# Cross-attention and FP8 layer on one core: ScalarE quantises the last three pieces, and TensorE turns the last four

## What is computed

```python
x = x + xattn(layernorm(x), ctx, ctx, ...)      # cross attention, an MLP of 512 hidden features, a layer norm
x = x + ffn(layernorm(x), weight, bias)         # one 128x128 layer; its input is rounded to 8-bit floats
...
f_diff = (v - attn @ v) @ W_diff.T + b_diff + q
h = layernorm(f_diff, ln_g, ln_b)
mlp = gelu(h @ W1.T + b1) @ W2.T + b2
out = layernorm(mlp + f_diff, ln_g, ln_b)
...
x_mat = quantize_e4m3(x2d).astype(float16)      # x2d: the second layer norm of the residual
out2d = x_mat @ w_mat.T + bias
```

## Time and profile before

| quantity | value |
|---|---|
| median of 3 runs | 262.22 us (261.59 to 262.32) |
| the profiled execution's own time | 262.39 us |
| its span in the trace | 260.6 us |
| VectorE busy | 225.0 us, 86% of the span |
| ScalarE busy | 214.1 us, 82% |
| TensorE matmuls busy | 209.4 us, 80% |
| GpSimd busy | 189.0 us, 73% |

### The profile page before, as it was taken

How to read it: one execution, slowest core, us unless ns; L and a number is a source line. 1 busy time by engine, 2 the same in 40 slices (tenths; PEclk the granted TensorE clock), 3 DMA queues, 4 the chain that set the end, 5 groups by cost and what they waited for, 6 DMA issues and landing times.

```text
span 260.6 us, 5926 instructions
## 1 busy us (share of the span) xinstructions
PE 209.4 (80%) x1723; PEld 178.2 (68%) x1723; DVE 225.0 (86%) x843; ACT 214.1 (82%) x774; POOL 189.0 (73%) x250
## 2 busy tenths in 40 slices
PE   2676696854499888887899999999999999996511
PEld 1754584633387666666699999999899999995400
DVE  2899999988879999999535889999999999999892
ACT  4599999998889999989997888989888776775431
POOL 2477666764899999991886796969697888666552
PEclk9999889895579999999999999999999999999855
DMA  5666554440000000000328189997978888977922
GB/s 146 193 201 192 171 150 136 144 118 1 1 0 3 3 0 3 1 3 4 40 26 95 19 96 135 122 132 111 149 117 132 131 123 127 140 121 121 103 62 60
DMA packets 51360, 23.65 MB, mean 91 GB/s; under 512 B 9856, under 2 KB 51200, under 8 KB 51328
## 3 DMA queue, kind: packets, MB, share of 16 engines
q0 software_dynamic: 15856, 7.87, 28.1%
q1 hardware_dynamic: 35040, 15.21, 21.8%
q10 hardware_dynamic: 432, 0.20, 0.4%
HBM read 9.37 MB, written 4.19 MB: 52 GB/s over the span
## 4 chain that ended last, share of the span: by engine, by line
POOL 28%; DVE 23%; ACT 20%; issue 13%; PE 11%; DMA 3%; SPq 0%; POOLq 0%; DVEq 0%; ACTq 0%
POOL F L407 7%; POOL xrstd L448 7%; ACT TQK L523 6%; ACT TQK L507 6%; POOL orstd L442 6%; DVE q_c L810 5%; POOL F L454 5%; DVE LN_c L818 5%; DVE F L838 5%; PE bank L1011 3%; ACT PV L518 3%; DMA LN_c<-in_ctx_dram 3%; ACT vT_c L512 2%; PE bank L960 1%; DVE F L863 1%
## 5 line engine op out<-in xcount | busy, mean ns | idle before, releaser
L1011 PEld LDWEIGHTS bank<-W2T,TQK 128*128 128x128 f32 x512 | 63.0, 191 | 6.7 <-DVE F L858 1.8
L1011 PE MATMUL bank<-W2T,TQK 128*128 128x128 f32 x512 | 64.8, 277 | 2.9 <-ACT TQK L545 2.9
L545 ACT ACTIVATE TQK<-bank,b1c 128x512 f32<-128x512 f32 (+1 forms) x68 | 42.8, 663 | 3.0 <-PE bank L1004 2.7
L448 POOL TENSOR_TENSOR xrstd<-xvar,pow_c 128x4 f32<-128x4 f32 (+1 forms) x17 | 18.6, 1092 | 22.6 <-DVE xvar L726 22.6
L362 POOL TENSOR_TENSOR xrstd<-xvar,pow_c 128x4 f32<-128x4 f32 x16 | 16.8, 1051 | 21.5 <-DVE xvar L726 21.5
L1002 PE MATMUL bank<-hTh,W1h 128*128 128x512 f32 (+1 forms) x68 | 30.0, 442 | 0.8 <-DVE hTl L801 0.8
L407 POOL DMA_DIRECT2D F<-rows x17 | 26.0, 1529 | 5.6 <-DVE E_c L796 5.6
L1003 PE MATMUL bank<-hTl,W1h 128*128 128x512 f32 (+1 forms) x68 | 26.0, 382 | 0.0
L1004 PE MATMUL bank<-hTh,W1l 128*128 128x512 f32 (+1 forms) x68 | 25.9, 381 | 0.0
L960 PE MATMUL bank<-WdT,vT_c 128*128 128x128 f32 x128 | 21.6, 321 | 4.5 <-ACT vT_c L512 4.3
L960 PEld LDWEIGHTS bank<-WdT,vT_c 128*128 128x128 f32 x128 | 18.8, 225 | 7.0 <-ACT vT_c L512 6.9
(11 more groups left out here) (129 smaller groups left out, 658.6 us busy)
## 6 DMA issues: line engine op xcount, KB each, us to landing
F<-rows POOLq DMA_DIRECT2D x29, 256.0 KB, 4.7
LN_c<-in_ctx_dram SPq DMA_DIRECT2D x16, 256.0 KB, 3.0
X<-in_x_dram SPq DMA_DIRECT2D x16, 256.0 KB, 3.2
out_dram<-F SPq DMA_DIRECT2D x15, 256.0 KB, 2.4
LN_c<-in_L_xattn_W_dram SPq DMA_DIRECT2D x1, 256.0 KB, 3.6
lT_c<-in_L_xattn_W_dram SPq DMA_DIRECT2D x1, 256.0 KB, 3.7
F<-rows POOLq DMA_DIRECT2D x2, 128.0 KB, 4.8
out_dram<-F SPq DMA_DIRECT2D x2, 128.0 KB, 1.8
```

Of the source, the lines that this page charges most:

```text
L448: pool.tensor_tensor(buf(xrstd, x1, G), buf(xvar, x1, G), pow_c[:, 0:x1.g], ALU.pow).then_inc(x1_rstd, 1)
L545: act.activation(hid(m, j), m1_bank(m, j), ACT.Gelu, bias=b1c[:, j:j + 1]).then_inc(gelu_ready, 1)
L1011: last = pe.matmul(M2_B[m.buf][:, i * D:(i + 1) * D], hid(m, j)[:, i * D:(i + 1) * D], W2T[:, j * D:(j + 1) * D], start=(j == 0 and i == 0 ...
```

## The change

Pieces 14 to 16 are quantised by ScalarE and not by VectorE: Identity with scale = rstd and bias = -mean * rstd, one activation a tile. The bias is made by a new GpSimd product `x1_shift` (into `nrden`, a buffer that is free in stage three, called `nmr`), behind each `x1_power`. VectorE's statistics of these pieces give the negative mean (`mean_sign` -1 in an operation that is there anyway). Two new semaphores, `xq_act` and `nmr_ready`, carry the new waits.

Piece 13 is turned by TensorE too (`XQ_HERE` goes from 14 to 13): its bf16 copy on ScalarE, its transposing DMA and the DMA's wait go. TensorE's turning now stands behind the MLP's products of the same step. It matters for piece 13 alone, since there is no MLP work in the later steps.

The new orders:

- ScalarE, last step: gelu(16, 0), gelu(16, 1), rounded(12), gelu(16, 2), gelu(16, 3), out_squares(15). After it: copy of turned 13, rounded(13), out_squares(16), quantise(14), copy of turned 14, quantise(15), rounded(14), copy of turned 15, quantise(16), rounded(15), copy of turned 16, rounded(16).
- VectorE, last step: output(15), residual(14), x1_stats(14), result(12). After it: output(16), residual(15), x1_stats(15), residual(16), x1_stats(16), result(13), result(14), result(15), result(16).
- GpSimd, last step: out_power(15). After it: x1_power(14), x1_shift(14), out_power(16), x1_power(15), x1_shift(15), add_bf(14), x1_power(16), x1_shift(16), add_bf(15), add_bf(16).

```diff
--- before.py
+++ after.py
@@ -91,7 +91,8 @@
     EARLY = 2
     NORMS = NC - 2
     BF_HERE = NP - 3
-    XQ_HERE = NP - 3
+    XQ_HERE = NP - 4
+    XQ_ACT = NP - 3
 
     with ExitStack() as ctx:
         def sb(name, shape, dt=F32):
@@ -174,6 +175,7 @@
         r16_c = LN_c[:, 2 * C:3 * C].bitcast(F16)
 
 
+        nmr = nrden
         qpart_c = RNORM[:, :]
         Wd_raw = E_c[:, 0:D]
         W1_raw, W1u = LN_c[:, 2 * C:2 * C + HB * D], LN_c[:, 3 * C:3 * C + HID]
@@ -289,6 +291,7 @@
             sem("x1_rstd"))
         xq_ready, xqT_ps, xqT_sb, ff_ps, r16_ready, y_ready = (
             sem("xq_ready"), sem("xqT_ps"), sem("xqT_sb"), sem("ff_ps"), sem("r16_ready"), sem("y_ready"))
+        xq_act, nmr_ready = sem("xq_act"), sem("nmr_ready")
         xq16_ready, xqT_in = sem("xq16_ready"), [sem(f"xqT_in{i}") for i in range(2)]
         stored, w1u_sb, wt_sb = sem("stored"), sem("w1u_sb"), sem("wt_sb")
 
@@ -444,12 +447,21 @@
 
             def x1_power(x1):
                 pool.wait_ge(x1_var, x1.n + 1)
-                wait(pool, xq_ready, x1.n - 1)
+                wait(pool, xq_ready, min(x1.n - 1, XQ_ACT))
+                wait(pool, xq_act, x1.n - 1 - XQ_ACT)
                 pool.tensor_tensor(buf(xrstd, x1, G), buf(xvar, x1, G), pow_c[:, 0:x1.g],
                                    ALU.pow).then_inc(x1_rstd, 1)
 
+            def x1_shift(x1):
+                pool.wait_ge(x1_rstd, x1.n + 1)
+                mv = xmv[:, x1.buf * G * 2:(x1.buf * G + x1.g) * 2].rearrange("p (t s) -> p t s", s=2)
+                pool.tensor_tensor(buf(nmr, x1, G), mv[:, :, 0], buf(xrstd, x1, G), ALU.mult).then_inc(nmr_ready, 1)
+
             def add_bf(x1):
-                pool.wait_ge(xq_ready, x1.n + 1)
+                if x1.n < XQ_ACT:
+                    pool.wait_ge(xq_ready, x1.n + 1)
+                else:
+                    pool.wait_ge(xq_act, x1.n - XQ_ACT + 1)
                 if x1.n < BF_HERE:
                     pool.dma_start(tiles(chunk(F, x1)), over_tiles(bf_r, x1.g),
                                    accum_op=ALU.add).then_inc(bf_added[x1.n % 3], 16)
@@ -470,12 +482,12 @@
                 if k.live and k.n > 0:
                     add_b2(k)
                 x1 = at(3)
-                if x1.live:
+                if x1.live and x1.n < XQ_ACT:
                     x1_power(x1)
                 o = at(2)
                 if o.live:
                     out_power(o)
-                if x1.live:
+                if x1.live and x1.n < XQ_ACT:
                     add_bf(x1)
                 v = at(-4)
                 if v.live and (v.n % 2 == 1 or v.n == NP - 1):
@@ -483,11 +495,17 @@
 
             norm_power(pieces[3])
             run_steps(pieces, 1, phase3)
-            out_power(pieces[NP - 1])
-            x1_power(pieces[NP - 2])
-            add_bf(pieces[NP - 2])
-            x1_power(pieces[NP - 1])
-            add_bf(pieces[NP - 1])
+            full, early, last = pieces[NP - 3], pieces[NP - 2], pieces[NP - 1]
+            x1_power(full)
+            x1_shift(full)
+            out_power(last)
+            x1_power(early)
+            x1_shift(early)
+            add_bf(full)
+            x1_power(last)
+            x1_shift(last)
+            add_bf(early)
+            add_bf(last)
 
 
         @block.scalar
@@ -646,11 +664,13 @@
                 q = at(5)
                 if q.live and q.n < XQ_HERE:
                     rounded(q)
-                if o.live:
+                if o.live and not is_piece(m, NP - 1):
                     out_squares(o)
                 if m.live and m.n > 0:
                     gelu(m, 2)
                     gelu(m, 3)
+                if is_piece(m, NP - 1):
+                    out_squares(o)
                 v = at(-4)
                 if v.live:
                     squares(v)
@@ -661,13 +681,35 @@
                     act.activation(buf(xq16_c, c), buf(xq_c, c), ACT.Copy).then_inc(xq16_ready, 1)
 
             run_steps(pieces, 1, phase3)
-            rounded(pieces[XQ_HERE - 1])
-            out_squares(pieces[NP - 1])
-            for q in pieces[XQ_HERE:]:
+
+            def quantise(q):
+                act.wait_ge(nmr_ready, q.n - XQ_ACT + 1)
+                wait(act, xqT_ps, q.n - 1 - XQ_HERE)
+                for i in range(q.g):
+                    at_i = q.buf * G + i
+                    last = act.activation(tile(xq_c, q, i), all_tile(F, q, i), ACT.Identity,
+                                          bias=nmr[:, at_i:at_i + 1], scale=xrstd[:, at_i:at_i + 1],
+                                          saturate=False)
+                last.then_inc(xq_act, 1)
+
+            def turned(q):
                 act.wait_ge(xqT_ps, q.n - XQ_HERE + 1)
                 wait(act, ff_ps, q.n - 1)
                 act.activation(buf(xqT_c, q), XQ_B[:, 0:q.g * D], ACT.Copy).then_inc(xqT_sb, 1)
-                rounded(q)
+
+            before, full, early, last = pieces[NP - 4], pieces[NP - 3], pieces[NP - 2], pieces[NP - 1]
+            turned(before)
+            rounded(before)
+            out_squares(last)
+            quantise(full)
+            turned(full)
+            quantise(early)
+            rounded(full)
+            turned(early)
+            quantise(last)
+            rounded(early)
+            turned(last)
+            rounded(last)
 
 
         @block.vector
@@ -711,13 +753,13 @@
                 dve.tensor_tensor(mv, st[:, :, 1:3], st[:, :, 4:6], ALU.add)
                 dve.tensor_tensor(gap, st[:, :, 1], st[:, :, 4], ALU.subtract).then_inc(halves, 1)
 
-            def stats_halves(k, halves, terms):
+            def stats_halves(k, halves, terms, mean_sign=1):
                 mv = xmv[:, k.buf * G * 2:(k.buf * G + k.g) * 2].rearrange("p (t s) -> p t s", s=2)
                 gap = buf(xgap, k, G)
                 dve.wait_ge(halves, k.n + 1)
                 dve.scalar_tensor_tensor(out=gap, in0=gap, scalar=0.25, in1=gap, op0=ALU.mult, op1=ALU.mult)
                 dve.tensor_scalar(mv[:, :, 1], mv[:, :, 1], 1.0 / D, LN_EPS, ALU.mult, ALU.add)
-                dve.tensor_scalar(mv[:, :, 0], mv[:, :, 0], 0.5, None, ALU.mult).then_inc(terms, 1)
+                dve.tensor_scalar(mv[:, :, 0], mv[:, :, 0], 0.5 * mean_sign, None, ALU.mult).then_inc(terms, 1)
 
             def stats_var(k, terms, done):
 
@@ -896,8 +938,9 @@
             def x1_stats(x1):
                 x1_moments(x1)
                 wait(dve, x1_rstd, x1.n - 1)
+                wait(dve, nmr_ready, x1.n - 1 - XQ_ACT)
                 stats_terms(x1, x1_bn, x1_halves)
-                stats_halves(x1, x1_halves, x1_terms)
+                stats_halves(x1, x1_halves, x1_terms, 1 if x1.n < XQ_ACT else -1)
                 stats_var(x1, x1_terms, x1_var)
 
             def phase3(at):
@@ -925,12 +968,10 @@
             output(last)
             residual(early)
             x1_stats(early)
+            residual(last)
+            x1_stats(last)
             result(pieces[NP - 4])
-            residual(last)
             result(full)
-            quantise(early)
-            x1_stats(last)
-            quantise(last)
             result(early)
             result(last)
 
@@ -1079,13 +1120,6 @@
                     pe.transpose(XQ_B[:, 0:D], wq[1], ident[:, :]).then_inc(wf_ps, 1)
                 if is_piece(q, 0):
                     pe.wait_ge(wf_sb, 1)
-                if q.live and q.n >= XQ_HERE:
-                    pe.wait_ge(xq_ready, q.n + 1)
-                    wait(pe, xqT_sb, q.n - XQ_HERE)
-                    for i in range(q.g):
-                        last = pe.matmul(XQ_B[:, i * D:(i + 1) * D], tile(xq_c, q, i), ident8[:, :],
-                                         start=True, stop=True)
-                    last.then_inc(xqT_ps, 1)
                 if m.live:
                     if m.n > 0:
                         mlp1(m, 2)
@@ -1094,6 +1128,16 @@
                     mlp2(m, 1)
                     mlp2(m, 2)
                     mlp2(m, 3)
+                if q.live and q.n >= XQ_HERE:
+                    if q.n < XQ_ACT:
+                        pe.wait_ge(xq_ready, q.n + 1)
+                    else:
+                        pe.wait_ge(xq_act, q.n - XQ_ACT + 1)
+                    wait(pe, xqT_sb, q.n - XQ_HERE)
+                    for i in range(q.g):
+                        last = pe.matmul(XQ_B[:, i * D:(i + 1) * D], tile(xq_c, q, i), ident8[:, :],
+                                         start=True, stop=True)
+                    last.then_inc(xqT_ps, 1)
                 if q.live and q.n < XQ_HERE:
                     pe.wait_ge(xqT_in[q.buf], 16 * (q.n // 2 + 1))
                 if q.live and q.n >= XQ_HERE:
```

## The result

The changed kernel takes 258.62 us (median of 4 runs, 258.23 to 258.91) against 262.18 us before. The ratio is 0.9869, with a 95% interval of 0.9848 to 0.989: 3.6 us faster. In a later comparison on one chip the same pair gave 0.9901 [0.9879 to 0.9924], 259.04 against 261.55: 2.5 us. The prediction was 259.4 us, 2.8 us faster, in a range of 257.8 to 261.0.

What follows compares the result with a forecast made beforehand. A chain of small operations strung on VectorE's written order bounds the end; variance(16) at 250.9 plus a 4.65 tail puts the last sum at 255.5, 2.8 us earlier, so 259.4 us, range 257.8 to 261.0.

Steps and rivals of the forecast that it cites:

- gelu(16, 0) starts: ScalarE's first Gelu of piece 16, freed of piece 13's copy and 2.83 us idle: at 239.1 instead of 240.81.
- MLP of 16 ends: Last second-product matmuls of piece 16 on TensorE: end at about 241.9, 2.4 us earlier.
- variance(15): End of VectorE's statistics of piece 15, behind residual(15): at 247.45, 3.0 us earlier.
- variance(16): End of VectorE's statistics of piece 16: at 250.9 instead of 254.6, 3.7 us earlier, with the collision charged.
- What bounds it: The end is a chain of small operations with VectorE's written order as backbone, not bound by throughput.
- The collision: GpSimd's add_bf(14), 1.26 us, holds VectorE's two-input L711 of piece 16: 1.0 us charged, between 0 and 1.3.
- The tail: From variance(16) to the last sum: 3.72 us, plus 0.37 for power, 0.3 for shift, 0.27 for ScalarE's pair, 4.65.
- Rival A: The add lands between VectorE's two-input operations, no collision: last sum at 254.1, time 258.1; chance 0.14.
- Rival B: GpSimd's powers hold VectorE's residual(15) and residual(16) while they run: about 1.1 us less gain, 260.5; chance 0.18.
- Rival C: ScalarE, taking all quantising, copies and roundings in one order, becomes the backbone: no gain, 262; chance 0.05.
- Rival D: ScalarE loads tables around each quantise, six loads of 1.28 us: slower, 265.6; chance 0.04.
- Rival E: A misplaced wait of the new orders, say output(16) on its DMA, keeps the tail: 261.5 to 263; chance 0.04.

Runs made afterwards that it cites:

- e1: Kernel before, with only piece 13's turn by TensorE added and VectorE still quantising in its old order: 262.34 us against 262.43, ratio 0.9993.
- e3: Changed kernel's orders, but VectorE quantises pieces 14 to 16 and GpSimd makes no shift: 260.73 us, ratio 0.9938 to before.
- e5: Changed kernel with GpSimd's sum of piece 14 moved behind the power and shift of piece 16: 258.11 us, ratio 0.9837 to before.
- e9: Changed kernel with GpSimd's sum of piece 14 cut in halves, the second behind the shift of 16: 257.52 us, ratio 0.9847 to before.
- e10: Changed kernel's orders with VectorE quantising pieces 14 to 16 and piece 14's bias added by DMA, not GpSimd: 259.48 us, ratio 0.9917 to before.
- e2: Changed kernel with piece 13 given back to ScalarE's bf16 copy and the transposing DMA: 259.87 us, ratio 0.9902 to before.
- e7: Changed kernel with the bias of piece 14 added by the adding DMA, not by a GpSimd sum: 259.43 us, ratio 0.9888 to before.

## Why the prediction was right

Its steps, measured from the power of piece 13 (predicted times less 237.99):

| step | predicted | measured |
|---|---|---|
| gelu(16, 0) starts | 1.1 | 0.98 |
| MLP of 16 ends | 3.9 | 3.98 |
| output(16) | 6.7 | 6.68 |
| variance(15) | 9.46 | 9.47 |
| GpSimd's sum of 14 | 10.9 to 12.2 | 10.5 to 11.8 |
| variance(16) | 12.9 | 12.42 |
| tail, variance(16) to the last sum | 4.65 | 4.74 |
| last sum | 17.5 | 17.16 |

- **What bounds it:** right. e1 lets gelu(16, 0) start 1.7 us earlier and gains nothing; e3 alters VectorE's order and leaves it the quantising, and gains 1.83. The order of VectorE is the backbone.
- **The collision:** right in place and kind, wrong in size. I charged 1.0 us, "rows 5 is the nearest case and waited in full"; it cost 0.54. From variance(15) to the sum's start I had 1.40 us and it was 1.05 (power(15) 0.74, the shift 0.20), so the sum ended 0.37 earlier than worked out; and from its end to variance(16) it was 0.63 and not 0.75. The sum's end, not its length, is what counts. Without the collision I had variance(16) at 11.9; e5 and e9, which remove it, have 11.89 and 11.88.
- **The tail:** the sum fits (4.65 and 4.74), two of its terms don't, and that they cancel is luck. I added 0.37 for the power and 0.3 for the shift. The power waited for nothing (0.72), since VectorE's result(13) came 0.27 us behind variance(16) and the power got in first. The shift waited 0.55 and put off quantise(16) by 0.72 in all. ScalarE's pair took 0.88, as L559 had it (0.87).
- **Rival A**, no collision: false as a forecast (L753 at 0.70). e9 takes the collision out and ends where this rival had it: its last sum at 254.1 is 16.1 behind the anchor, and e9 has 16.06.
- **Rival B**, powers hold VectorE: false. The power of 247.08 lies on both tiles of residual(16), which take 0.61 as undisturbed, and the sum of 247.56 starts while it runs and takes 0.42 as elsewhere; the power itself took 0.74. By the Trainium skill, page SBUF — State Buffer, section "SBUF: two separate sides", a GpSimd operation that starts first has the shared pair for the whole instruction. The sums of L469 do so here; the small powers don't.
- **Rival C**, ScalarE as backbone: false; it waited for the shift of 16 (1.32 us idle ahead of quantise(16)). **Rival D**, table loads: false; the profile has the same three loads as before, none in the stretch. **Rival E:** false; output(16) came at 6.68 where I had 6.7, and the last sum 3.19 earlier.
- **ScalarE's taking over** is worth more than I thought. For e3 I expected 0.3 to 1.0 us, and it was 1.36. e3 and e10 show why: a quantise on VectorE is held by GpSimd's sum and one on ScalarE isn't, and without the sum 0.75 of the 1.36 go. The prediction didn't have that part.
- **Medians:** 3.6 us against the stretch's 3.2 in the first comparison, 2.5 in the second. The stretch is the steadier measure; that the remainder is variation of the stages ahead is argued from their unaltered orders, not shown.

## What to carry to other kernels

When a chain of small operations ends a kernel, find the engine whose written order strings it together, and ask of each operation there whether the last chain needs it; letting another engine go ahead earlier (e1: 1.7 us) can be worth nothing until that is done, and something (e2: 0.7 us) afterwards. A GpSimd sum of two tensors placed beside VectorE work cost up to 0.9 us of its 1.26 (rows 5, e3); put it beside VectorE's `bn_stats` (L916), which it doesn't hold, or cut it, so that its end falls where VectorE's next held operation begins. Moving it wholly behind the chain (e5) gave 0.58 us where cutting it (e9) gave 1.10, since result(14) then waits longer for it (1.41 against 0.88) and rounded(16) waits for result(14).

## What the runs showed of the hardware

- GpSimd's sum of 128x512 held a VectorE quantise with one tensor input (1.23 us for 0.34, e3), not only operations with two. `bn_stats` of 128x128 was not held (0.49 for two tiles beside L469 after and beside L475 in e9, as in the earlier trace rows). The Trainium skill, page SBUF — State Buffer, section "Who interferes with whom", says that a tensor_scalar can enter a mode in which it takes the pair shared with GpSimd; e3 agrees in the hold; no row tells whether the tile was in that mode.
- GpSimd is held too: a power that meets a VectorE sum under way takes 1.40 for 1.03 (243.76), a shift 0.75 for 0.20. A power already under way isn't held and holds nobody (residual(16), 0.61).
- Behind the issue of an adding DMA, the next power on GpSimd took 1.45 us instead of 0.7 (e7). By the times, VectorE's result(13) of 250.19 did most of it: the power ended as if begun 0.13 us ahead of result(13)'s end, and the powers that meet a sum in before (244.23) and in e3 (252.26) ended as if begun 0.15 and 0.13 ahead of its end. The issue lasted until 250.21, so it can have kept the power of 250.00 from getting in first. This is argued, not tried.
- Beside that issue VectorE's L761, with one tensor input, took 0.32 for 0.16 (e7), and quantise(15) 0.75 for 0.60 (e10), while L753, with two, kept its 0.16. That the issue is the cause was not tried.
